# A two-layer decoder block on one core: routing selection ahead of a gate, constant matmuls in TensorE's waits, casts at the end of the first tile

## The reference, cut to what matters

```python
x = x + tanh(g_xattn[0]) * cross_attention(layernorm(x), mask, ctx)         # 32 heads of 8, rotary, plus adapter attention on ctx
x = x + tanh(g_ffn[0])   * moe_top1(layernorm(x), wg, W, b)                 # 8 experts of 256 x 256, softmax gate
x = x + tanh(g_xattn[1]) * wkv(w, u, layernorm(x), ctx)                     # a recurrence along the 64 positions
x = x + tanh(g_ffn[1])   * moe_top2(layernorm(x), w_gate, w1, w2, w3)       # 8 experts, silu(x w1) * (x w3), then w2, inner size 704
```

## Time and profile before

| | us |
|---|---|
| median of 3 runs | 542.29 |
| lowest, highest | 541.72, 549.66 |
| the profiled execution's own time | 543.49 |
| its span, first to last instruction | 541.6 |
| PE busy | 476.9 (88%) |
| DVE busy | 392.6 (72%) |
| ACT busy | 263.7 (49%) |
| POOL busy | 169.7 (31%) |
| mean granted PE clock | 0.954 of full |

### The profile page before, as it was taken

One profiled execution on the slowest core, in us unless ns is written; L12 is line 12 of the kernel. 1 busy time (PEld: TensorE's weight loads), 2 busy tenths in 40 slices (PEclk: granted clock), 3 DMA queues, 4 the chain that ended last, 5 costly groups with the idle time before them and its releaser, 6 DMA issues. The chain is left out here.

```text
span 541.6 us, 10345 instructions
## 1 busy us (share of the span) xinstructions
PE 476.9 (88%) x3090; PEld 355.0 (66%) x3091; DVE 392.6 (72%) x1042; ACT 263.7 (49%) x562; POOL 169.7 (31%) x228
## 2 busy tenths in 40 slices
PE   4589999999989988988988859877889999999994
PEld 2458678667567576675776636545568788878782
DVE  4856878788897897888987777937676566556640
ACT  2546283374462662743731432511646666666651
POOL 4150204114113123141131143220345556555622
PEclk9888997999999999999998958988999999999997
DMA  7921304004004004022040179553657667767721
GB/s 239 278 42 21 62 3 79 5 23 79 5 21 79 15 10 77 24 38 45 21 80 6 39 301 422 201 159 128 229 146 232 206 204 230 249 208 195 232 27 21
DMA packets 24755, 63.38 MB, mean 117 GB/s; under 512 B 5161, under 2 KB 15281, under 8 KB 21777
## 3 DMA queue, kind: packets, MB, share of 16 engines
q1 hardware_dynamic: 19440, 56.38, 33.9%
q0 software_dynamic: 4416, 6.03, 6.1%
q10 hardware_dynamic: 864, 0.54, 0.3%
HBM read 48.79 MB, written 5.24 MB: 100 GB/s over the span
## 5 line engine op out<-in xcount | busy, mean ns | idle before, releaser
L1901 PE MATMUL bank_o<-w,hT 128*128 (+1 forms) x276 | 70.4, 398 | 1.1 <-DVE hT L1323 0.7
L1337 DVE TENSOR_TENSOR wl<-lw,wh 128x1024 fp32r<-128x1024 f32 (+1 forms) x54 | 60.9, 1129 | 0.3 <-ACT wh L621 0.3
L1901 PEld LDWEIGHTS bank_o<-w,hT 128*128 128x128 f32 (+1 forms) x276 | 50.4, 195 | 15.6 <-issue 10.0
L494 POOL TENSOR_SCALAR rstd<-mv 128x1 f32<-128x1 f32 x32 | 7.2, 225 | 168.4 <-DVE mv L956 168.4
L1028 DVE TENSOR_REDUCE mx<-bank_s 128x8 f32<-128x512 f32 x64 | 43.3, 686 | 14.7 <-PE bank_s L1645 14.2
L621 ACT ACTIVATE wh<-lw 128x1024 fp32r<-128x1024 f32 (+1 forms) x54 | 53.0, 981 | 0.0
L1643 PE MATMUL bank_s<-Kh,Qx 128*128 128x128 f32 x256 | 43.2, 293 | 4.6 <-DVE mx L1028 3.3
L1330 DVE TENSOR_TENSOR hh<-sg,bank_s 128x256 f32<-128x256 f32 x46 | 19.1, 418 | 35.9 <-ACT sg L849 26.8
L1643 PEld LDWEIGHTS bank_s<-Kh,Qx 128*128 128x128 f32 x256 | 37.1, 202 | 7.5 <-DVE mx L1028 4.0
L575 POOL DMA_INDIRECT out_x<-ys,idx_out x18 | 29.0, 1609 | 37.6 <-ACT ys L860 36.8
L662 ACT ACTIVATE Qx<-qs,CN 128x512 fp32r<-128x512 f32 x56 | 35.2, 710 | 5.5 <-DVE qs L1001 5.4
(11 more groups left out here) (346 smaller groups left out, 1157.3 us busy)
## 6 DMA issues: line engine op xcount, KB each, us to landing
lw<-in_w SPq DMA_DIRECT2D x18, 1408.0 KB, 6.5
Q<-Qx SPq DMA_DIRECT2D x16, 512.0 KB
up<-in_w SPq DMA_DIRECT2D x5, 1408.0 KB, 6.9
w<-in_w SPq DMA_DIRECT2D x4, 1536.0 KB, 11.8
Pt<-in_WT SPq DMA_DIRECT2D x1, 1024.0 KB, 11.8
X<-in_x SPq DMA_DIRECT2D x1, 896.0 KB, 8.3
CT<-in_ctxT SPq DMA_DIRECT2D x1, 896.0 KB, 8.7
out_x<-X SPq DMA_DIRECT2D x6, 128.0 KB, 1.7
```

What stands on the lines that cost most here:

```text
L1337: dve.tensor_tensor(wl[par][:, :, at:at + k], lw[par][:, :, at:at + k], wh[par][:, :, at:at + k].bitcast(F32), ALU.subtract).then_inc(w_lo, 1)
L1901: ins = pe.matmul(bo[:, 0:HID], hT[0:k, i, :], w2[0:k, bass.ts(e, 1), i, :].rearrange("p o n -> p (o n)"), start=(i == 0), stop=(i == IT - 1))
```

## The change

It has four parts. In tile 0, DVE takes the first two maxima and the layer norm of tile 1 ahead of the `Kl` casts, and the constants of the routing go to the tile's end; POOL's second and third subtraction wait until DVE has rotated tile 1's keys (`k_rot`). `warm` is called with 3 and 4 in place of 1 and 2. In the tail, PE issues nine constant matmuls ahead of `turn_heads(u)`, `early_up(0, 0)` ahead of `turn_h2(u)`, `early_rows(2)` behind `turn_h(1)` and `turn_y(u - 1)`, and `early_up(2, 2)` ahead of `turn_y(u)`. DVE takes `early_weights_in` ahead of `gates(1, ...)`, `wkv_out(u)` ahead of `ln_stats(3, w)`, and `select(T1, NT)` ahead of `gates(3, 0)`; ACT takes `h_turned(3)` ahead of `gates(4, 0)` and the first weight copy.

```diff
@@
                     pool.wait_ge(w0_hi, i + 1)
+                    if i == 1:
+                        pool.wait_ge(k_rot, 2 * BT)
                     pool.tensor_tensor(w0l[:, c, e:e + n, :], raw, w0h[:, c, e:e + n, :].bitcast(F32), ALU.subtract).then_inc(w0_lo, 1)
@@
             scaled(2, 0)
+            h_turned(3)
             gates(4, 0)
             high_w(N1, N1 % 2, 0)
-            h_turned(3)
             high_w(N1, N1 % 2, 1)
@@
             low_k(0, 0)
-            dve.memset(ys[0][:, :], 0.0).then_inc(zr, 1)
+            maxima(0, range(1))
             dve.wait_ge(ld_x, 16 * 2)
+            ln_stats(0, 1)
+            maxima(0, range(1, 2))
+            ln_apply(0, 1)
             for i in range(2):
...
                                 CN[S:P, C_ONE:C_ONE + P].rearrange("p (o k) -> p o k", o=1).to_broadcast([S, BT * G, P])).then_inc(prep, 1)
-            dve.tensor_copy(posb[:, :], CN[:, C_POS:C_POS + P]).then_inc(routeb, 1)
-            dve.tensor_copy(trib[:, :], CN[:, C_TRI:C_TRI + P]).then_inc(routeb, 1)
-            dve.tensor_copy(ttb[:, :], CN[:, C_TT:C_TT + TOPK * NT]).then_inc(routeb, 1)
-            dve.tensor_copy(ttb1[:, :], CN[:, C_TT1:C_TT1 + TOPK * T1]).then_inc(routeb, 1)
-            dve.tensor_copy(idb[:, :], ident).then_inc(routeb, 1)
-            dve.memset(onesb[:, :], 1.0).then_inc(routeb, 1)
-            ln_stats(0, 1)
-            maxima(0, range(1))
-            ln_apply(0, 1)
-            maxima(0, range(1, 2))
+            dve.memset(ys[0][:, :], 0.0).then_inc(zr, 1)
             dve.wait_ge(prep_act, 2)
 
-            def negated():
+            def constants_of():
+                dve.tensor_copy(posb[:, :], CN[:, C_POS:C_POS + P]).then_inc(routeb, 1)
+                dve.tensor_copy(trib[:, :], CN[:, C_TRI:C_TRI + P]).then_inc(routeb, 1)
+                dve.tensor_copy(ttb[:, :], CN[:, C_TT:C_TT + TOPK * NT]).then_inc(routeb, 1)
+                dve.tensor_copy(ttb1[:, :], CN[:, C_TT1:C_TT1 + TOPK * T1]).then_inc(routeb, 1)
+                dve.tensor_copy(idb[:, :], ident).then_inc(routeb, 1)
+                dve.memset(onesb[:, :], 1.0).then_inc(routeb, 1)
                 dve.wait_ge(ld_small, 16 * 6)
@@
                 if not prev:
-                    negated()
+                    constants_of()
 
@@
             wkv_args(u)
+            early_weights_in()
             gates(1, 0)
...
             gates(1, 2)
-            early_weights_in()
             wkv_products(dve, u)
...
             wkv_inverse(u)
+            wkv_out(u)
             ln_stats(3, w)
-            wkv_out(u)
             gates(2, 0)
@@
             gates(2, 2)
+            select(T1, NT)
             gates(3, 0)
-            select(T1, NT)
             gates(3, 1)
@@
                     if first and b == 1:
-                        warm(1)
+                        warm(3)
                     after(pe, k_rot, t, BT, b + 1)
@@
 
+            def constant_products(o, n):
+
+                for i in range(n):
+                    pe.matmul(o[:, :], Idup[:, :], w0h[:, 0, 0:2, :].rearrange("p e n -> p (e n)"), start=True, stop=True)
+
             def gate_logits(u, o=bt[1]):
@@
             pe.wait_ge(prep, 2)
-            warm(2)
+            warm(4)
             pe.wait_ge(zeroed, 10)
@@
             after(pe, p_exp, u, 8, 8)
+            after(pe, mix_step, u - 1, 5 + E0, 5 + E0)
+            constant_products(bt[0], 9)
             turn_heads(u, False, bt[1])
@@
             after(pe, x1_in, u, 1, 1)
+            early_up(0, 0)
             turn_h2(u)
-            early_up(0, 0)
             gate_logits(u, bb)
@@
             early_down(0, e)
-            early_rows(2)
             turn_h(1)
...
             turn_y(u - 1, bt[1])
+            early_rows(2)
             early_up(2, 0)
             early_up(2, 1)
+            early_up(2, 2)
             turn_y(u, bt[0])
-            early_up(2, 2)
             pe.wait_ge(x3_in, u)
```

## The result

The changed kernel took 548.87 us (median of four: 547.19, 548.82, 548.92, 551.31) against 542.0 of the kernel before beside it: a ratio of 1.0133 with a 95% interval of 1.0085 to 1.0182. In twelve more executions, of which the first experiment tells, the ratio was 1.0057 (0.9998 to 1.0115), so the loss of this first measurement is larger than that of the sixteen together. The ratios leave out each execution more than 1.5% above the fastest of the same kernel, which here drops the 549.66 of the kernel before and nothing of the changed one; the plain means of the four and four give 1.0097. The forecast was 536.8, with a range that ended at 541.2. The sign was wrong, and the range missed.

The account below looks back on a forecast made before the run. PE alone was taken to bound the kernel from 404 us on, so only the even slots' start could move. +2.7 - 1.5 - 2.8 - 3.9 = -5.5 took 543.49 to 538.0, or 536.8 as median; range 531.2 to 541.2.

Parts of the forecast that it names:

- The held cast: Tile 0: POOL's subtraction holds the second `Kl` cast, so the fifth unit starts at 31.3, a loss of 3.3 us.
- From the fifth unit to `turn_q`: Tile 0: the fifth unit's +3.3 us carries over, less 1.4 for the query rotation, so `turn_q` moves by +1.9.
- The sentence on the clock: Tile 0: ACT's chain from `turn_q` to the first exponentials hides PE's clock, so no gain was taken.
- the low end: Tile 0 with casts not held: `turn_q` moves by -2.9 us, tile 0 by -2.1; as rival 532.0 us, chance 0.24.
- The constants: End of tile 0: six constants now stand ahead of tile 2's norm and tile 1's third maximum, costing 0.8 us.
- Tile 0 as a whole: All of tile 0's changes together: a loss of 2.7 us, or -2.1 at best.
- The rotation: Tile 0: POOL's later subtractions wait for `k_rot`, so tile 1's query rotation keeps its 0.43 us, a gain of 1.40.
- Tail, first part: Constant matmuls and `early_up(0, 0)` in PE's waits bring the gate's logits earlier: -1.5 us, bounds -0.7 and -2.4.
- The rival in which the constant matmuls do not lift the clock: Tail: the clock stays at half, so the tail gives only 5.2 us; 539.8 us, chance 0.17.
- Tail, second part: `early_up(2, 2)` no longer follows `turn_y(u)` and twelve matmuls run faster: -2.8 us, bounds -1.5 and -3.1.
- Tail, third part: DVE's selection ends before `turn_h(2)`, PE loses its 2.93 us wait, the table comes earlier: -3.9 us, low end -2.4.
- A gather behind one more load: Slot 7's gather lands behind one more weight load of 6.5 us: sum +1.0, 543.3 us, chance 0.05.

Follow-up runs that it names:

- the first experiment: The changed kernel once more with no edit, twelve executions: median 548.92 us, ratio 1.0057 against the kernel before.
- free casts: The changed kernel with POOL's first subtraction also waiting until both `Kl` casts are done, run twice: medians 538.88 and 539.97 us, ratios 0.9957 and 0.9895.
- after: The changed kernel itself, in its first measurement's profiled execution: 547.19 us.
- tile0_again: The kernel before with only the edits of tile 0, run again: 555.49 us beside 542.46 for the kernel before.
- after_again: The changed kernel run again with no edit: median 548.92 us, ratio 1.0057 against the kernel before.
- tile0_only: The kernel before with only the edits of tile 0, `k_rot` and longer `warm` calls included: median 545.15 us, ratio 1.0046.
- constants_late: The kernel before with the tail's edits, `k_rot` in POOL's second subtraction and the six routing constants at tile 0's end: median 541.62 us, ratio 0.9915.
- tail_only: The kernel before with only the edits of the tail: median 543.38 us, ratio 0.9943.

## Why the prediction was wrong, by its steps

- **The held cast: right, and it was the forecast's own case.** The second cast ran from 24.44 to 29.43 and ended 0.55 behind the subtraction. The first cast took 0.69 as ever; the subtraction began 0.09 behind it and took 4.96 in place of 4.52. The Trainium skill (SBUF — State Buffer, Who interferes with whom) says that a cast can use the port pair that DVE shares with GpSimd, and that whichever of the two is issued first then blocks the other. This trace agrees: 5.60 in place of 1.29, the same in all four traces with that order. The fifth unit was 2.40 later (30.42 against 28.02) although the first scores had begun 0.74 earlier, so 3.1 against the 3.3 forecast.
- **From the fifth unit to `turn_q`: the step that failed.** The forecast carried the fifth unit's +3.3 over to `turn_q` unchanged ("`turn_q` (38.60) moves by +3.3 - 1.4 = +1.9"), so PE's clock in between was a term put at nothing without a reason. The sentence on the clock, that ACT's chain hides it, speaks only of the time behind `turn_q`. In between, PE's work took 9.49 in place of 6.74, 2.7 us more, at half clock. `turn_q` came 3.7 later (4.5 with the earlier start) and not 1.9, and in the three other traces with held casts 3.6 to 4.2. It would have failed with free casts too: there `turn_q` came 0.3 to 0.6 earlier, and not the 2.9 of the low end. So this loss did not hang on how long PE had idled. In after and tile0_again the clock fell at 22.7 and 23.2, ahead of the 5.8 us, in after_again and tile0_only inside it; with 1.82 us idle the loss was the same. In the kernel before the clock was back at 30.8; what decides when it comes back stays open.
- **The constants: 0.6 and not 0.8.** In all seven traces in which they moved, DVE loses 0.64 to 0.65 between 50 and 54 us, and in none of the others. Where they had stood, the third unit came 0.6 sooner (constants_late), and the runs show nothing of either.
- **Tile 0 as a whole.** It came out 5.0 to 7.2 behind in four traces, mean 6.0. The six traces with the old tile 0 (0 to +2.3, mean 1.3) show that some of this is the luck of the trace I started from; the difference, 4.7, stands against the forecast's 2.7. In the runs it is 6.1 ± 2.5, and 3.2 ± 0.5 at equal clock: the forecast's waits were nearly right and the clock was missing. Free casts took 8.3 off the mean, of which 2.4 at equal clock.
- **The rotation: right.** 0.41 in the trace, and 1.5 in the runs.
- **The middle tiles: not a term at all.** The sum was made against one profiled execution, and its middle had 13.7 us at half. Of the seventeen other traces one had as little, sixteen had 23.9 to 54.6, and the same instructions took up to 13.3 longer, in the five other traces whose program is the old one up to the tail as well (+8.9, +8.8, +11.3, -0.1, +9.8). Part of that is that profiled executions are mostly slow ones; but this one's clock, 0.954, lay above its kernel's mean of 0.947, which by the line is 2.6 us. Its own time did not show this: at 543.5 it lay near the median, with a kind middle and 20.5 at half in its tail. In the changed kernel's profiled execution the middle cost 3.7. The range had nothing for it.
- **Tail, first part: right.** DVE came back from 8.7 behind at 313 to 7.1 at 325 (-1.6; forecast -1.5), and 9.71 us of PE work in the stretch ran at full clock. The rival in which the constant matmuls do not lift the clock is refuted: 13.7 to 17.1 us at half behind that place in the six traces without them, 3.4 to 6.8 in the twelve with them.
- **Tail, second part: right on PE in this trace, not borne out as time.** From 7.1 to 4.5 behind at 365.29, the transposes for the router logits (-2.6; forecast -2.8, where its three terms add to -2.7). But PE's edits alone gave 1.0 ± 1.2 in the mean and cost 0.9 ± 0.4 at equal clock, and the whole tail gave 0.3 ± 0.5 more than the selection alone: of the 4.3 of the first two parts no run shows more than what the clock gives.
- **Tail, third part: right in its mechanism, not in this execution.** The selection left the path, but the clock fell for `early_up(3, 0)` (6.59 in place of 3.68), and 0.8 came of 3.9. In after_again the whole tail gave 8.2, the forecast's number, and 7.6 to 9.6 in seven others (tail_only: 6.3). The forecast took the kernel before's tail as it stood, with 20.5 at half; in two other traces (tile0_only, tile0_again, 17.1 and 20.5 at half) the old tail was itself 0.4 to 2.4 shorter, and in the runs the tail gives 4.6 ± 1.6, and 3.6 at equal clock, of the 8.2. Some 3.3 of the 8.2 were gains of clock by the forecast's own terms: 0.8 in the first part (its bound at half throughout was -0.7), 0.67 in the second and 1.80 in the third.
- **A gather behind one more load:** did not happen.

By place, then, the profiled execution missed by +2.3 in tile 0, +3.7 in the middle and +3.2 in the tail: 9.2, from 538.0 to 547.2. In each of the three the rows show half clock where the loss is: behind the fifth unit, in the middle's stretches, and in `early_up(3, 0)`. For the middle's share I take luck: no edit stands there, and the five traces with the old program up to the tail spread from -0.1 to +11.3. The other executions lay 1.6 to 4.1 above that, at clocks of 0.925 to 0.938. What stays open: why half clock lasts until 35 us and more in all six traces with tile 0's new order, held casts or free, and in two of the twelve with the old; where the 0.016 of mean clock between held and free casts lies, since in the two traces with free casts neither the stretch from the fifth unit to `turn_q` nor the middle is better; and what sets the middle's stretches in one execution.

## What to carry to other kernels

Price the work of PE behind a wait at both clocks, and ask which of them the trace at hand shows: here the same work took 5.4 to 9.6 us. Do not make a sum against one profiled execution when executions differ by more than the sum: first ask how much half clock that one had, and in which stretches. A gain read on one engine's timeline in one trace is not yet time: try the piece alone. And when DVE work moves, look at what POOL does at the new time: the same two casts cost 1.3 or 5.6 us by what stood beside them.

## What I had not expected of the hardware

- The time of all these kernels follows the mean granted clock closely: 3.76 us for each 0.01, over 229 executions, with 1.34 us left over.
- With identical instructions the middle tiles (252 us) had 13.7 to 54.6 us at half clock and took up to 13 us more.
- The four traces in which PE idles 5.8 to 6.1 us in tile 0 had 17 to 24 us at half there, those with the old order 7 to 20. Twelve `warm` calls in idle time of 2.8 us left none.
- Nine matmuls ahead of the tail went with 3.4 to 6.8 us at half in the next 30 us in twelve traces of twelve; without them it was 13.7 to 17.1 in six of six.
- POOL also lost time to the casts: its subtraction took 4.96 beside them and 4.52 behind them.
